# A fused state-space and feed-forward layer on one core: first and last norm in halves, rotating buffers for the last projection

## The reference

```
x = x + attn(layernorm(x));  x = x + ffn(layernorm(x))
attn: zxbcdt = u @ W_in.T             (z0, x0: 512 columns each; xBC: 544; dt: 8)
      xBC = silu(causal depthwise conv of width 4 over tokens)
      scan over tokens, 8 heads of 64, state 16:
          h = exp(dt*A)*h + dt * x outer B;   y = h.C + D*x
      y = layernorm(y)*gamma+beta;  y = sigmoid(y @ W_gate.T + b_gate) * y
      out = concat[silu(z0)*x0, y] @ W_out.T
ffn:  h = gelu(x @ T(W_fc).T);  h = layernorm(h)*ln_w + ln_b;  out = h @ T(W_proj).T
      (T: ternary weights; hidden width 1024)
```

## Time and profile before

| | us |
|---|---|
| median of 3 runs | 1140.49 (1139.97 to 1142.7) |
| the profiled execution, its time | 1140.65 |
| the profiled execution, its span | 1138.9 |
| PE busy in the span | 1070.2 (94%) |
| DVE, ACT, POOL busy | 980.7, 956.6, 456.3 |
| PE's first instruction begins at | 17.64 |
| ACT's last instruction ends at | 1129.17 |

### The profile page before, as it was taken

One profiled execution on the slowest core, in us unless ns is written; L12 is line 12 of the kernel. 1 busy time (PEld: TensorE's weight loads), 2 busy tenths in 40 slices (PEclk: granted clock), 3 DMA queues, 4 the chain that ended last, 5 costly groups with the idle time before them and its releaser, 6 DMA issues. The chain is left out here.

```text
span 1138.9 us, 23206 instructions
## 1 busy us (share of the span) xinstructions
PE 1070.2 (94%) x8310; PEld 681.9 (60%) x8310; DVE 980.7 (86%) x1963; ACT 956.6 (84%) x1686; POOL 456.3 (40%) x564
## 2 busy tenths in 40 slices
PE   3788999999999999999999999999999999999985
PEld 1464656466675666657575665656666566757563
DVE  5999998899898988988889997999988888787664
ACT  5877678899889988797999998889798988888755
POOL 1123244433533544363443615254261533453631
PEclk9889999999999999999999999999999999999999
DMA  6522334453444345445435455353626344443565
GB/s 194 165 57 47 86 57 67 74 94 84 94 94 87 74 91 114 94 89 105 82 87 98 85 110 104 86 101 68 120 49 124 72 95 66 94 84 84 100 133 111
DMA packets 306562, 105.93 MB, mean 93 GB/s; under 512 B 275344, under 2 KB 302736, under 8 KB 306448
## 3 DMA queue, kind: packets, MB, share of 16 engines
q1 hardware_dynamic: 306448, 104.46, 45.1%
HBM read 24.32 MB, written 8.39 MB: 29 GB/s over the span
## 5 line engine op out<-in xcount | busy, mean ns | idle before, releaser
L364 PE MATMUL bank<-xnT,win 128*128 128x512 f16 (+1 forms) x1248 | 299.6, 387 | 24.0 <-DMA xnT<-hb 17.9
L364 PEld LDWEIGHTS bank<-xnT,win 128*128 128x128 f16 (+1 forms) x1248 | 122.2, 102 | 159.3 <-issue 29.1
L973 DVE SCALAR_TENSOR_TENSOR cv<-bank,cws,cv 128x510 f32<-128x510 f32 (+5 forms) x240 | 176.8, 744 | 11.6 <-ACT tail L688 4.3
L364 PE MATMUL bank<-yhl,wg 128*128 128x512 f16 x768 | 172.3, 380 | 3.3 <-DMA yhl<-ynh 2.5
L182 ACT ACT_TABLE_LOAD x127 | 162.9, 1283 | 3.0 <-PEq L1429 0.7
L1245 POOL TENSOR_TENSOR cat<-sz,cat 128x512 f16<-128x512 f32 x64 | 79.4, 1244 | 157.1 <-ACT cat L802 157.1
L1241 POOL TENSOR_TENSOR caty<-tg,caty 128x512 f16<-128x512 f32 x64 | 81.8, 1287 | 141.7 <-ACT caty L790 141.7
L595 PE MATMUL bank<-wpj,hT 128*128 128x256 f16 x1024 | 123.1, 275 | 13.1 <-DMA hT<-hb 11.9
L364 PEld LDWEIGHTS bank<-yhl,wg 128*128 128x128 f16 x768 | 74.4, 98 | 92.6 <-issue 4.1
L583 PE MATMUL bank<-wfc,x3T 128*128 128x512 f16 x512 | 122.9, 380 | 3.0 <-DMA x3T<-hb 1.7
L595 PEld LDWEIGHTS bank<-wpj,hT 128*128 128x128 f16 x1024 | 99.1, 98 | 35.7 <-issue 12.9
(11 more groups left out here) (148 smaller groups left out, 2066.5 us busy)
## 6 DMA issues: line engine op xcount, KB each, us to landing
x<-in_x SPq DMA_DIRECT2D x32, 512.0 KB, 4.1
out_y<-x SPq DMA_DIRECT2D x15, 512.0 KB, 3.1
crep<-cv SPq DMA_DIRECT2D x128, 32.0 KB, 2.0
hT<-hb SPq DMA_TRANSPOSE x128, 3.2
caty<-in_wg SPq DMA_DIRECT2D x1, 1024.0 KB, 7.0
x<-in_wout SPq DMA_DIRECT2D x1, 1024.0 KB, 6.3
hT<-in_wfc SPq DMA_DIRECT2D x1, 1024.0 KB, 9.7
hb<-in_wpj SPq DMA_DIRECT2D x1, 1024.0 KB, 6.0
```

What stands on the lines that cost most here:

```text
L364: m = eng.matmul(b, lhs(p, k), rhs(q, k), start=(n == 0), stop=(n == len(seq) - 1))
L973: op = eng.scalar_tensor_tensor(cs[0:w, j, 3 - k:T], b[0:w, 0:T - 3 + k], cws[0:w, j, k:k + 1], cs[0:w, j, 3 - k:T], ALU.mult, ALU.add)
```

## The change

1. Block 0's first norm goes in two halves of two chunks: x is loaded by two DMAs, and `var_x`, `norm_x`, `half_x`, `rest_x` and `turn_x` run once for each half. The products still wait for all of it.
2. Block f's second norm goes in two halves likewise. `fc` of chunks 0 and 1 needs the first half alone, `fc` of chunks 2 and 3 the second as well.
3. `half_h`, `rest_h` and `turn_h` of the last two blocks take other buffers for some chunks: `halves[0]` for chunks 1 and 3 of block e and chunk 1 of block f, `halves[2]` for chunk 2 of block f. The wait is for the last user of the same buffer.
4. `cum` becomes two products of full width in place of eight narrow ones.
5. All five order strings are new, from the first word to the last, for all 16 blocks.

The core of the diff (the orders, and the same edit on the other engines, are left out):

```diff
 PE_ORDER = (
...
-    "of5 pe7 pe1 ff3 ff6 ff4 ff2 ff5 pe0 ff7 ff3 ff6 pf4 pf2 pf1 pf0 "
...
+    "ff6 pe4 ff7 ff5 ff1 pe0 ff3 pe2 ff6 pf7 pf5 pf1 pf3 "
...
+        def part(i, n, halved):
+            return slice(2 * n, 2 * n + 2) if i == halved else slice(0, NCH)
+        LATE = {(LAST - 1, 1): 0, (LAST - 1, 3): 0, (LAST, 1): 0, (LAST, 2): 2}
+        def h_halves(i, c):
+            return LATE.get((i, c), 1)
+        def before(i, c):
+            at = 4 * i + c
+            return next((q for q in range(at - 1, -1, -1) if h_halves(q // 4, q % 4) == h_halves(i, c)), None)
...
             def cum(i, n, at):
-                for c in range(NCH):
-                    for q in range(2):
-                        m = eng.matmul(b[32 * c:32 * c + 32, 0:P], ahl[:, i % 2, q, c, :], upto, start=(q == 0),
-                                       stop=(q == 1), skip_group_check=True)
+                for q in range(2):
+                    m = eng.matmul(b[:, 0:P], ahl[:, i % 2, q, :, :].rearrange("p c r -> p (c r)"), upto, start=(q == 0),
+                                   stop=(q == 1))
...
             def fc(i, n, at):
                 pe.wait_ge(x3t_hi, 16 * (i + 1))
                 pe.wait_ge(x3t_lo, 16 * (i + 1))
+                if i == LAST and c >= 2:
+                    pe.wait_ge(x3t_hi2, 16)
+                    pe.wait_ge(x3t_lo2, 16)
...
             def half_x2(i, n):
-                act.wait_ge(x2_out, 4 * i + 4)
+                cs = part(i, n, LAST)
+                act.wait_ge(x2_out, 4 * i + cs.stop)
...
             def half_h(i, c):
-                if at:
-                    act.wait_ge(hn_lo, at)
-                    act.wait_ge(ht_hi[(at - 1) % 2], 16 * ((at - 1) // 2 + 1))
-                eng.activation(halves[1][:, 0, :], h[:, at % 3, :], ACT.Copy).then_inc(hn_hi, 1)
+                last = before(i, c)
+                if last is not None:
+                    act.wait_ge(hn_lo, last + 1)
+                    act.wait_ge(ht_hi[last % 2], 16 * (last // 2 + 1))
...
+                eng.activation(halves[h_halves(i, c)][:, 0, :], h[:, at % 3, :], ACT.Copy).then_inc(hn_hi, 1)
...
-            load_x(0)
+            eng.dma_start(x[:, 0:2, :], x_v[0][:, 0:2, :]).then_inc(ld_x0, 16)
+            eng.dma_start(x[:, 2:4, :], x_v[0][:, 2:4, :]).then_inc(ld_x, 16)
...
-            def turn_x2(i, n):
+            def turn_x2(i, m):
+                n, q = m // 2, m % 2
+                cs = part(i, n, LAST)
                 sp.wait_ge(fc_mm, 8 * i)
-                sp.wait_ge((x2_hi, x2_lo)[n], i + 1)
-                eng.dma_start(x3T[:, n, :, :, :].rearrange("p c k t -> p (c k) t"), halves[2][:, n, :], transpose=True
-                              ).then_inc((x3t_hi, x3t_lo)[n], 16)
+                sp.wait_ge((x2_hi, x2_lo)[q], x2_steps(i, n))
+                eng.dma_start(x3T[:, q, cs, :, :].rearrange("p c k t -> p (c k) t"), halves[2][:, q, cols(cs)],
+                              transpose=True).then_inc(((x3t_hi, x3t_lo), (x3t_hi2, x3t_lo2))[n][q], 16)
```

More of the change, by code:

```diff
@@ L646, in norm_x @@
             def norm_x(i, n):
-                act.wait_ge(x_nm, 3 * i + 3)
-                for c in range(NCH):
+                cs = part(i, n, 0)
+                act.wait_ge(x_nm, 3 * x_steps(i, n))
+                for c in range(cs.start, cs.stop):
                     op = eng.activation(x[:, c, :], x[:, c, :], ACT.Identity, scale=rs1[:, c:c + 1],
@@ L664, in half_x2 @@
                 act.wait_ge(gam_v, 3)
-                eng.activation(halves[2][:, 0, :], x2[:, i % 2].rearrange("p c d -> p (c d)"), ACT.Copy
+                eng.activation(halves[2][:, 0, cols(cs)], x2[:, i % 2, cs].rearrange("p c d -> p (c d)"), ACT.Copy
                                ).then_inc(x2_hi, 1)
@@ L939, in bias_out, with variance @@
                 eng.tensor_copy(r0[:, :], b[:, 0:DM]).then_inc(r0_v, 1)
-            def variance(src, st, mv, rs):
-                for c in range(NCH):
+            def variance(src, st, mv, rs, cs):
+                for c in range(cs.start, cs.stop):
                     op = eng.bn_stats(st[:, c, :], src[:, c, :])
                 then(op)
-                for c in range(NCH):
+                for c in range(cs.start, cs.stop):
                     op = eng.bn_aggr(mv[:, c, :], st[:, c, :])
@@ new lines, in var_x @@
+                if i:
+                    dve.wait_ge(x_var, x_steps(i - 1))
+                variance(x, st1, mv1, rs1, part(i, n, 0)).then_inc(x_var, 1)
+            def rest_x(i, n):
+                cs = part(i, n, 0)
+                dve.wait_ge(xn_hi, x_steps(i, n))
+                if i:
+                    dve.wait_ge(xt_lo, 16 * x_steps(i - 1))
+                eng.tensor_tensor(halves[0][:, 1, cols(cs)], x[:, cs, :].rearrange("p c d -> p (c d)"),
+                                  halves[0][:, 0, cols(cs)], ALU.subtract).then_inc(xn_lo, 1)
@@ L1142, in var_x2 @@
             def var_x2(i, n):
-                dve.wait_ge(x2_out, 4 * i + 4)
+                cs = part(i, n, LAST)
+                dve.wait_ge(x2_out, 4 * i + cs.stop)
                 dve.wait_ge(x2_var, i)
                 dve.wait_ge(gelu, 8 * i)
-                variance(x2[:, i % 2], st3, mv3, rs3).then_inc(x2_var, 1)
+                variance(x2[:, i % 2], st3, mv3, rs3, cs).then_inc(x2_var, 1)
             def centre_h(i, c):
@@ L1163, in rest_h @@
                 at = 4 * i + c
+                hh = halves[h_halves(i, c)]
                 dve.wait_ge(hn_hi, at + 1)
-                if at:
-                    dve.wait_ge(ht_lo[(at - 1) % 2], 16 * ((at - 1) // 2 + 1))
-                eng.tensor_tensor(halves[1][:, 1, :], h[:, at % 3, :], halves[1][:, 0, :], ALU.subtract
-                                  ).then_inc(hn_lo, 1)
+                last = before(i, c)
+                if last is not None:
+                    dve.wait_ge(ht_lo[last % 2], 16 * (last // 2 + 1))
+                elif h_halves(i, c) == 0:
+                    dve.wait_ge(xt_lo, 16 * x_steps(LAST))
+                elif h_halves(i, c) == 2:
+                    dve.wait_ge(x3t_lo, 16 * (i + 1))
+                    dve.wait_ge(x3t_lo2, 16)
+                eng.tensor_tensor(hh[:, 1, :], h[:, at % 3, :], hh[:, 0, :], ALU.subtract).then_inc(hn_lo, 1)
             def add_ffn(i, c):
@@ L1247, in norm_x2 @@
             def norm_x2(i, n):
[L1248 to L1249 removed]
+                pool.wait_ge(x2_var, x2_steps(i, n))
+                power(rs3[:, part(i, n, LAST)]).then_inc(x2_rs, 1)
             def add_bias(i, n):
                 xi = x2[:, i % 2]
[L1253 to L1254 removed]
+                pool.wait_ge(x2_lo, x2_steps(i, n))
+                pool.wait_ge(x2_rs, x2_steps(i, n))
                 pool.wait_ge(r0_v, 1)
[L1256 removed]
+                for g in (n,) if i == LAST else range(2):
                     op = eng.tensor_tensor(xi[:, 2 * g:2 * g + 2, :], xi[:, 2 * g:2 * g + 2, :],
@@ L1359, in turn_h @@
                 sp.wait_ge((hn_hi, hn_lo)[q], at + 1)
-                eng.dma_start(hT[:, c % 2, q, :, :], halves[1][:, q, :], transpose=True
+                eng.dma_start(hT[:, c % 2, q, :, :], halves[h_halves(i, c)][:, q, :], transpose=True
                               ).then_inc((ht_hi, ht_lo)[q][c % 2], 16)
```

95 lines of the change are left out of this document (54 added, 41 removed), and 236 rows, old and new, of tables (ACT_ORDER, DVE_ORDER, PE_ORDER, POOL_ORDER).

## The result

The changed kernel takes 1127.85 us (median of 4 runs, 1126.84 to 1132.95) where the kernel before took 1141.03 beside it: ratio 0.9896, 95% interval 0.9866 to 0.9925. Run again in a later set it gave 0.9893 [0.9876, 0.991]. The forecast of 1128.8 lies 1 us from the median; the parts from which it was summed fit less well, and most of what follows is about them.

What follows compares the result with a forecast made beforehand. PE was taken as the bound (busy 1070.2 of 1138.9 us), with DVE setting the pace until 120 us. Terms 1.7 + 1.5 + 5.9 + 2.6 = 11.7 us off 1140.65 gave 1128.95, or 1128.8 beside the median; range 1123.5 to 1136.5.

Steps and rivals of the forecast that it cites:

- The start: Block 0's first norm in halves: first product earlier than 17.64 us, 1.7 us gained, bounds 0 and 3.0.
- rival that halves bring nothing: Both halved norms: half-size transposes cost as much as full ones, start gives 0, second norm 3.5; 1132.9 us, chance 0.17.
- `cum`: Two full-width products replace eight narrow ones in each of 16 blocks: 1.5 us gained, bounds 0 and 1.8.
- The end: Last two blocks: 5.9 us from block f's second norm in halves plus 2.6 us from the additional buffers.
- The first term: Block f's second norm in halves: first gelu 6.9 us earlier, less about 1.0, so 5.9 us, bounds 3 and 7.
- signs named for the end: Gelu 3 us behind output product, no ACT wait over 1 us for `hT`, back-to-back last transposes, PE busy 23 us.
- Next in line is DVE: Block f's last chunk: without ACT's 4.17 us buffer wait, DVE's lo copy, then SP's queue, bind; 2.6 us gained.
- The orders: New order strings, all blocks: ACT loses 12.8 us of table loads; taken as 0, bounds 3 gained and 6 lost.
- DVE sets the pace: From 17.64 to 120 us, DVE works 95.08 of 102.36 us and PE 86.69, so DVE was taken as the bound.
- the turn of y runs out of cover: Rival, blocks 2 to 4: less PE work hides y's transposes, some 24 us of stalls, 1153 us; chance 0.06.
- given back in the middle: Rival, middle or prologue: terms hold by half (6 us), new order costs 4, 1138.5 us; chance 0.09.
- ACT did keep up with block e: Rival: ACT late with block e's work; judged to fit, 11.6 us within 17 us of PE work; no separate chance.

Runs made afterwards that it cites:

- typical profile: Second profiled execution of the changed kernel, no edit, from its repeat in a later set: 1126.96 us; that set's median was 1126.52 us, ratio 0.9893.
- the second halving without rotation: Changed kernel with the last two blocks' gelu outputs and halves back in two buffers, two order steps moved ahead: 1139.31 us, 0.9991 to the kernel before.
- rotation alone: Kernel before plus only the other buffers for the last two blocks' projection halves; old orders, narrow products, whole norms: 1139.78 us, 1.0005.
- first profile: First profiled execution of the changed kernel, no edit: 1132.95 us, 5 us more than the median.

## Why the prediction came out right, and where it was wrong

The typical profile is 13.7 us shorter than that of before (1140.65 to 1126.96), where 11.7 was forecast; the medians differ by 13.2 and 12.9.

**The start: forecast 1.7, measured 0.18 and 0.35, and none of it due to the halves,** since the first product comes as early with the norm whole. This step failed. It said that "the queue time should scale and the way there and back should not". The runs show nearly the reverse: the queue time doesn't scale at all, and the flight shortens by 0.7 us, more than the 0.4 assumed. The profile of before did bound it ("It can need as long as a full one"), and the value was taken from the wrong end: four issues 1.31 apart from 10.66 put the last at 14.59, 2.6 in flight make it 17.19, and 17.29 was measured. The rule weighed there, from the page "DMA: Bandwidth & Descriptors" of the Trainium skill (section "Anatomy of one DMA"), would take 0.3 us off a half's flight; the measured 0.7 is more than twice that. The 1.31 us for which each issue holds SP's queue are no term of that rule, and they decided. Nor did block 1's x come earlier. The rival that halves bring nothing was right for the start, and for SP's queue at both ends.

**`cum`: forecast 1.5 of a possible 1.8, measured 0.12 us in the block that was looked at, which for 16 blocks would be 1.9.** The occupation was read rightly. That it comes off the whole time isn't shown: the run with narrow `cum` doesn't resolve it.

**The end: forecast 8.5 in two terms, measured 8.0 as one.** The first term's mechanism holds: no wait of the first `fc`, 0.5 us for the second half's, gelu 2.65 us behind the output product, which is 7.1 us earlier than before where 6.9 was forecast. From that gelu to the span's end it is 28.8 us (29.7 before), 0.9 us less, where the forecast has 1.6: 2.6 for the buffers less the 1.0 that eats into the 6.9. Part of the 0.9 is in no term: one projection of the kernel before ran at the lower clock there (3.48 us), and none did in the kernel after. Two of the signs named for the end failed: SP's last four transposes aren't back to back, as SP waits for chunk 1's projection between them, and in the last 30 us PE works for 20.6, where 23 were expected. The split into 5.9 and 2.6 doesn't hold: as parts they were priced one by one, each against the profile of before. Alone, rotation gives 0 (1.0005), and the second halving without rotation, in the new orders, gives 0 too (0.9991) or even loses 3 us in the end; with the other in place, and in those orders, each is worth 8 to 11 us. The step that failed is "Next in line is DVE", and SP behind it: next in line behind ACT's buffer is `hT`, two buffers that PE must leave. It is worth 0.9 us with rotation alone, and 0.9 in the kernel after, where SP is done with chunk 2 at 1121.1 and issues chunk 3 at 1122.00. Two more things were taken as fixed and weren't. PE's clock was lower over the first `fc` products with rotation alone, which fits the other 1.4 us that were lost there. And "the 3.23 in flight" that "stay" don't: with destinations of their own, single transposes take 4.7 and 4.9 us, and nothing is gained that can be measured. What the other buffers do is not at the place of the 4.17 us wait, but 20 us earlier, where they keep ACT's queue moving, so that the second norm's copies aren't held behind block e's. That the two terms summed to the right number is luck.

**The orders: forecast 0, about 3.5 left over.** From the first product to the end of the last output product (before less one projection) it is 1081.9 us before and 1076.5 now, 5.4 less; `cum` may be 1.9 of that. One profile of each is a rough measure: two more kernels in the old orders have 1080.2 and 1080.6 there, all edits in the old orders 1078.0, and nine profiles in the new ones 1074.5 to 1077.3, the first profile's 1082.3 left aside. So the new orders are ahead, but by how much of the 3.5 isn't shown. It isn't in the 18.9 us of the middle, which stayed (18.3): there the forecast was right. It is ahead of 120 us, where PE idles 4.9 us less and pays, by an estimate, 2.0 back, since the mean granted clock there is 0.88 and not 0.90 of 102 us. The forecast read "DVE sets the pace" there and took it for a bound; DVE is busier by 2.4 us in that stretch now, so its idle time was to be had too. By the medians of the run in the old orders the new ones are worth 7.2 us, more than this remainder and the 1.9 of the end together; that isn't resolved either. How much of the 7.2 us between old and new orders with all edits comes from which string wasn't tried.

**The rivals.** Slower, as the turn of y runs out of cover, didn't happen: PE's waits for `yhl` don't stand among the longest of the stretch from 120 to 1040 us, and in blocks 2 to 4 they sum to 0.5 us. The length of the chain was not fixed. (Its "some 2 us of flight" are short: the transposes of y in the kernel before take 3.2 us, so the old order didn't quite cover the chain either.) Nothing was given back in the middle. ACT did keep up with block e; where it doesn't, without rotation, that rival is what one gets.

So 11.7 against 13.7: 1.4 too much for the start, 0.5 too much for the end, 0.4 too little for `cum` if all of it counts, and 3.5 too little for the orders, which is the remainder and not a measurement.

## What to carry to other kernels

Where two edits meet in one engine's queue, their worth is not a sum: price the second in the order that the first one leaves, and look for what stands behind a waiting instruction, not only at how long it waits. A ring of buffers is as deep as its shallowest stage, so count the destination's buffers along with the source's. Splitting a transfer pays only if the issuing queue has room for the additional issues; where the flight's start is behind a queue, fewer and larger ones are as early.

## What the runs showed of the hardware that I had not expected

- At both ends of the program a DMA transpose within SBUF mostly holds SP's queue for 1.19 to 1.36 us, for 128x512 and for 128x1024 float16 alike; the two of 128x2048 held it for 1.9 and 2.5. In flight they take 2.4 to 2.6, mostly 3.1 to 3.4, and 4.4 to 4.8 us. The full-size ones that took 3.7 to 4.9 us there stand next to block e's store of 512 KB in four kernels, but two of the kernel before (4.0 and 3.8) don't, and one of rotation alone (3.19) does, so the cause stays open.
- Eight products with a stationary operand of 32 columns hold PE for 0.23 us, and two of 128 columns for 0.11: each narrow one took 0.029 us and each full one 0.057, so the narrow ones must have overlapped, and still four of them cost twice what one full product of the same work does.
- At the end of the program PE's clock counts beside its waits: 16 products take 1.91 us at full clock and 2.56 to 3.57 us in some places behind waits of 1.3 to 3.4 us. Like waits elsewhere left it at full clock (2.03 and 1.45 us in the kernel after, run again; 2.52 and 2.76 in the kernel before), so what tells these apart isn't settled here.
